# Attention scores from two-part float32r queries and keys, two heads per instruction pair, in a one-core attention and expert kernel

## The chip, the cores and the metric

The kernel runs on one core of one Trainium2 chip, in one launch. The metric is the device time of that core in microseconds (us), the median of a few runs. TensorE (PE) multiplies matrices, VectorE (DVE), ScalarE (ACT) and GpSimd (POOL) work on elements, SyncE (SP) issues most transfers. All data is float32 in DRAM unless said.

## The reference, cut to what matters

A token lookup, a layer norm, multi-head attention with a rotary part, a residual, and a layer with 32 experts of which each token takes one. The change is in how queries and keys are stored, and in the scores and their maxima:

```
query = heads(ct_q @ Wu_q_w + Wu_q_b) + heads(_rope(ct_q @ Wq_r_w + Wq_r_b, cos, sin))
key   = heads(ct_kv @ Wu_k_w + Wu_k_b) + heads(_rope(x @ Wk_r_w + Wk_r_b, cos, sin))
attn  = softmax(einsum('bhqd,bhkd->bhqk', query, key) / scale)
out   = einsum('bhqk,bhkd->bhqd', attn, value)
```

There are 4 sequences of 2048 tokens, 256 channels, and 16 heads of 16 channels each. The scores of one head are a 2048 by 2048 matrix whose inner dimension is only 16.

## The kernel before

Four phases follow each other. Phase A (lookup, norm, queries, keys, values) works in 16 chunks of 512 tokens. Phase B is the attention. Phase C is the output product, the second norm and the router; phase D the experts. The order of instructions on each engine is written out by hand, and semaphores join the engines. The change touches A and B.

**Phase A.** For each chunk PE makes the rotary part (`rotary`, L290 and L293), the latents of the next chunk (`latent`, L276) and the content part (`content`, L302). DVE adds them into `full` (L412), once for queries and once for keys. `full` is then split into three bf16 numbers whose sum is the float32 number: ACT rounds it to bf16 (L358), POOL subtracts that from `full` to give `rest` (L250), ACT rounds the rest (L360), and DVE subtracts again (`third`, L417). SP stores the three parts to DRAM (L192), six transfers for queries and six for keys per chunk.

**Phase B.** The unit of work is 4 heads (a quad) with 512 queries. For each unit the product runs over 16 blocks of 128 keys. One block for the 4 heads is called a group here: there are 8 units in a step and 8 steps, so 1024 groups, each with 4 tiles of 128 keys by 512 queries. Per group:

- `scores` (L718), 4 matmuls, one per head, bf16: the keys of a block are the stationary operand, the queries stream through. The exact float32 product is had from six products of bf16 parts (`PAIRS`), which stand one above another in the contraction: 6 times 16 rows, and 3 more rows that carry the negative maximum of each query, so 99 rows in all. The result goes to one of three PSUM banks `ps_s`.
- ACT takes the exponential of each tile (L791) out of `ps_s` into `probs`.
- `weigh` (L733), 4 float32 matmuls, one per head, each in its own 32 columns of the array: values by `probs`, added up in the bank `ps_o`. PE carries out a float32 matmul as two instructions, so the trace shows 8.
- `maximum` (L698), 4 matmuls, bf16, 96 rows: the same scores turned round, queries stationary, for the maxima of a unit further on; DVE takes the maximum over the 512 keys (L813) out of one of three banks `ps_m`. The maxima run `LEAD` = 80 tiles ahead of the scores.

Once per unit DVE joins the maxima (L821), POOL splits them in three bf16 parts (L647 to L653), PE transposes them (`turn`, L708) into a bank of its own, `ps_n`, ACT copies them out (L774), and SP writes them into three rows of the queries. Once per unit ACT also copies `ps_o` out (L780).

PE goes through its program in order, and a matmul waits until the bank that it writes is free. The order within a group is: score, maximum, score, maximum, and so on four times, then the `weigh` of the group before.

Of the kernel before, what the change touches and what calls it, by code (L numbers as in the profile page):

```python
# [7 lines left out]
F32 = mybir.dt.float32  # L21
BF16 = mybir.dt.bfloat16
# [5 lines left out]
P = 128  # L28
# [17 lines left out]
PAIRS = [(0, 0), (0, 1), (0, 2), (1, 0), (1, 1), (2, 0)]  # L46
SROWS = len(PAIRS) * HD
MROWS = SROWS + PARTS
QUAD = 4
# [22 lines left out]
def phase_a(nc, dram, out):  # L72

    with ExitStack() as ctx:
# [30 lines left out]
        rest = sb("rest", [P, 2, 2, CH])  # L105
        parts = sb("parts", [P, 2, 2, PARTS, 2, CH], BF16)
# [28 lines left out]
        part1_ok = [sem("part1_ok_q"), sem("part1_ok_k")]  # L135
        rest_ok = [sem("rest_ok_q"), sem("rest_ok_k")]
        part2_ok = [sem("part2_ok_q"), sem("part2_ok_k")]
        part3_ok = [sem("part3_ok_q"), sem("part3_ok_k")]
# [5 lines left out]
        STORES = 2 * 2 * PARTS  # L144
# [9 lines left out]
        with nc.Block() as block:  # L154
            @block.sync
            def _(sp):
# [14 lines left out]
                def chunk(b, k, last):  # L171
# [15 lines left out]
                    for x in range(2):  # L187
                        sp.wait_ge(part3_ok[x], after(b, k))
                        for g in range(PARTS):
                            for eo in range(2):  # L190
                                dst = dram["qk"][x][bass.ds(b * HEADS, HEADS), g, eo, :, k * CH:(k + 1) * CH]
                                sp.dma_start(dst, parts[:, par, x, g, eo, :]).then_inc(parts_out[par], 16)  # L192
# [13 lines left out]
            def _(pool):  # L206
# [25 lines left out]
                def chunk(b, k, last):  # L232
# [13 lines left out]
                    for x in range(2):  # L246

                        pool.wait_ge(part1_ok[x], after(b, k))
                        pool.wait_ge(part3_ok[x], b * CPB + k)
                        pool.tensor_tensor(rest[:, x], full[:, x], parts[:, k % 2, x, 0], ALU.subtract).then_inc(rest_ok[x], 1)  # L250
# [87 lines left out]
            def _(act):  # L338
# [15 lines left out]
                def split(b, k, x):  # L354
# [24 lines left out]
            def _(dve):  # L379
# [26 lines left out]
                def add_content(b, k, x):  # L406
# [3 lines left out]
                    dve.wait_ge(rest_ok[x], b * CPB + k)  # L410
# [20 lines left out]
                def chunk(b, k, first, last):  # L431
# [3 lines left out]
                    if not (first and k == 0):  # L435

                        third(*((b, k - 1) if k else (b - 1, CPB - 1)), 1)
# [18 lines left out]
                    third(b, k, 0)  # L456
                    add_content(b, k, 1)

                bv_twice = b_v[:].rearrange("p (a h d) -> p a h d", a=1, d=HD).to_broadcast([P, 2, HEADS, HD])
                for k in range(CPB):  # L460
                    chunk(0, k, True, False)
                with dve.Fori(1, BATCH - 1) as b:
                    for k in range(CPB):
                        chunk(b, k, False, False)
                for k in range(CPB):
                    chunk(BATCH - 1, k, False, True)
                third(BATCH - 1, CPB - 1, 1)


def phase_b(nc, dram, out):  # L470
# [3 lines left out]
    TILES = UNITS * KT * QUAD  # L474
    PER_UNIT = KT * QUAD
    STEPS = QUADS // 2
    LEAD = PER_UNIT + 16
# [3 lines left out]
    QT = CH // P  # L481
    KC = SEQ // 512

    with ExitStack() as ctx:
# [5 lines left out]
        keys = sb("keys", [P, 2, QUAD, SEQ], BF16)  # L490
# [52 lines left out]
        def total(ring):  # L543

            return [len(range(i, TILES, ring)) for i in range(ring)]

# [1054 lines left out]
```

## Time and profile before

| | |
|---|---|
| time, median of 3 runs | 3951.06 us (3947.47 to 3952.72) |
| profiled execution, its own time is its span | 4004.2 us |
| PE busy | 3682.7 us, 92% |
| DVE busy | 3108.8 us, 78% |
| ACT busy | 2340.3 us, 58% |
| phase A | from 0 to about 380 us |
| phase B | from about 380 to about 3400 us |
| phases C and D | the rest, about 600 us |

The profile is of one execution, which took 53 us longer than the median of the runs without a profile. "Busy" for PE takes in the model of how a matmul drains; two matmuls overlap in the trace, so the time from the start of one to the start of the next is the better measure of pace.

### The profile page before, as it was taken

The numbers are of one execution on the slowest core, as the hardware profiler recorded it, in microseconds if no ns is written. First come the engines' busy times: TensorE is split into PE (matmuls) and PEld (weight loads), VectorE is DVE, ScalarE is ACT, GpSimd is POOL, SyncE is SP. The second block draws the span as 40 slices with busy tenths as digits, with TensorE's granted clock in tenths as the row PEclk, the third lists the DMA queues.
The fourth block names the chain that finished last, engine by engine and source line by source line (L and its number), as shares of the span: only waits on it lengthen the run. The fifth ranks groups of instructions, "written<-read, shape, count | busy, mean of one in ns | idle before, by whom it ended". The sixth has DMA issues, their size and how long they took to land. (4 is left out here: it accounts for less than half of the span.)

```text
span 4004.2 us, 70540 instructions
## 1 busy us (share of the span) xinstructions
PE 3682.7 (92%) x19328; PEld 1342.4 (34%) x19328; DVE 3108.8 (78%) x5336; ACT 2340.3 (58%) x4484; POOL 646.8 (16%) x838
## 2 busy tenths in 40 slices
PE   6775999999999999999999999999999999575888
PEld 3432233323323322333233323322332332464555
DVE  6887988888888888888888888888888885575222
ACT  2322477777767776777677767767777777100111
POOL 5554000000000000000000000000000000355554
PEclk9887799999999999999999999999999999776999
DMA  5556202020202111120202020202112000466442
GB/s 152 171 161 170 42 22 50 21 54 13 55 13 57 26 44 38 30 44 24 45 27 54 12 55 12 54 13 59 29 38 44 23 15 15 137 198 190 146 141 85
DMA packets 268209, 258.28 MB, mean 65 GB/s; under 512 B 59140, under 2 KB 225581, under 8 KB 267601
## 3 DMA queue, kind: packets, MB, share of 16 engines
q1 hardware_dynamic: 252496, 224.42, 22.0%
q0 software_dynamic: 15360, 29.50, 2.6%
q8 instruction: 180, 2.95, 0.3%
q14 instruction: 173, 1.41, 0.1%
HBM read 159.56 MB, written 103.49 MB: 66 GB/s over the span
## 5 line engine op out<-in xcount | busy, mean ns | idle before, releaser
L813 DVE TENSOR_REDUCE max_parts<-ps_m 128x1 f32<-128x512 f32 x4096 | 2546.0, 683 | 394.2 <-PE ps_m L698 392.3
L791 ACT ACTIVATE probs<-ps_s 128x512 f32<-128x512 f32 x4096 | 2129.3, 603 | 811.9 <-PE ps_s L718 811.7
L698 PE MATMUL ps_m<-keys,queries 96*128 96x512 bf16 x4096 | 1580.7, 386 | 33.3 <-DMA queries<-split_q 32.9
L718 PE MATMUL ps_s<-queries,keys 99*128 99x512 bf16 x4096 | 1564.4, 383 | 31.5 <-issue 25.4
L733 PE MATMUL ps_o<-probs,vals 128*32 128x512 f32 x8192 | 1094.7, 606 | 0.3 <-ACT weighted L780 0.2
L718 PEld LDWEIGHTS ps_s<-queries,keys 99*128 99x128 bf16 x4096 | 397.1, 97 | 1301.8 <-issue 819.7
L698 PEld LDWEIGHTS ps_m<-keys,queries 96*128 96x128 bf16 x4096 | 400.0, 98 | 474.2 <-DVE max_parts L813 92.5
L659 POOL TENSOR_TENSOR heads_out<-weighted,recip_rows 128x512 f32<-128x512 f32 x64 | 81.3, 1270 | 2103.1 <-DMA recip_rows<-recip_rows_dram 2103.1
L733 PEld LDWEIGHTS ps_o<-probs,vals 128*32 128x32 f32 x8192 | 161.4, 108 | 371.3 <-issue 356.5
L1509 DVE TENSOR_TENSOR hidden<-ps_u,silu 128x320 f32<-128x320 f32 x64 | 30.9, 491 | 178.3 <-PE ps_u L1445 131.3
L647 POOL TENSOR_TENSOR neg_split<-neg_max,zeros_b 128x16 bf16<-128x16 f32 x64 | 14.1, 220 | 771.3 <-DVE neg_max L821 771.3
L1103 PE MATMUL ps_p<-w_o,att_t 128*128 128x256 f32 x256 | 88.8, 522 | 34.4 <-DMA att_t<-att 30.4
L1488 ACT ACTIVATE silu<-ps_g 128x320 f32<-128x320 f32 x64 | 27.2, 436 | 146.1 <-PE ps_g L1445 110.9
L268 PE MATMUL ps_t<-ident_a,normed 128*128 128x128 f32 x128 | 28.7, 398 | 84.5 <-DVE normed L394 84.5
L1156 ACT ACTIVATE rows_t<-ps_tc 128x1024 f32<-128x1024 f32 x16 | 16.4, 1023 | 144.9 <-PE ps_tc L1113 106.6
L1455 PE MATMUL ps_y<-w_down,hidden 128*64 128x256 f32 x640 | 92.1, 386 | 8.8 <-DVE hidden L1509 8.8
L250 POOL TENSOR_TENSOR rest<-full,parts 128x1024 f32<-128x1024 f32 x32 | 68.2, 2130 | 140.5 <-ACT parts L358 140.2
L1404 POOL DMA_INDIRECT out<-result,tokens_d x80 | 80.1, 1001 | 46.1 <-DVE result L1516 34.1
L1388 POOL DMA_INDIRECT rows_d<-rows,tokens_d x80 | 80.9, 1012 | 35.9 <-issue 22.3
L1482 ACT ACTIVATE rows_td<-ps_td 128x512 f32<-128x512 f32 (+1 forms) x48 | 24.7, 525 | 106.0 <-PE ps_td L1434 64.0
L1103 PEld LDWEIGHTS ps_p<-w_o,att_t 128*128 128x128 f32 x256 | 68.8, 276 | 50.3 <-issue 36.1
L1445 PE MATMUL ps_g<-rows_td,w_gate 128*128 128x320 f32 x256 | 84.6, 478 | 0.6 <-issue 0.6
(103 smaller groups left out, 1931.7 us busy)
## 6 DMA issues: line engine op xcount, KB each, us to landing
queries<-split_q SPq DMA_DIRECT2D x384, 64.0 KB
rows<-rows_c SPq DMA_DIRECT2D x16, 1032.0 KB, 6.4
vext<-val SPq DMA_DIRECT2D x64, 256.0 KB, 3.6
vals<-vext SPq DMA_DIRECT2D x32, 512.0 KB
recip_rows<-recip_rows_dram SPq DMA_DIRECT2D x64, 256.0 KB
att<-heads_out SPq DMA_DIRECT2D x64, 256.0 KB, 2.7
split_q<-parts SPq DMA_DIRECT2D x96, 128.0 KB
split_k<-parts SPq DMA_DIRECT2D x96, 128.0 KB
```

The costliest lines, as they stand in the source:

```text
L250: pool.tensor_tensor(rest[:, x], full[:, x], parts[:, k % 2, x, 0], ALU.subtract).then_inc(rest_ok[x], 1)
L659: pool.tensor_tensor(heads_out[:, lu % 2, :], weighted[:, lu % 2, :], recip_rows[:, lu % 2, :], ALU.mult).then_inc(heads_ok, 1)
L698: pe.matmul(ps_m[bank][:], queries[0:SROWS, par, qt, j, t * P:(t + 1) * P], keys[0:SROWS, par, j, c * 512:(c + 1) * 512], start=True, stop ...
L718: pe.matmul(ps_s[n % BANKS][:], keys[0:MROWS, par, j, k * P:(k + 1) * P], queries[0:MROWS, par, qt, j, :], start=True, stop=True).then_inc ...
L733: mm = pe.matmul(ps_o[32 * j:32 * j + 32, :], vals[:, par, k, VW * j:VW * (j + 1)], probs[:, (n + j) % RING, :], start=k == 0, stop=k == K ...
L791: act.activation(probs[:, n % RING, :], ps_s[n % BANKS][:], ACT.Exp, scale=SCALE).then_inc(probs_ok[n % BANKS], 1)
L813: dve.tensor_reduce(max_parts[:, lu % 2, g:g + 1], ps_m[bank][:], AX.X, ALU.max).then_inc(maxima_ok[bank], 1)
L1103: mm = pe.matmul(ps_p[:, t // 2, t % 2 * DM:(t % 2 + 1) * DM], att_t[:, k % 2, d, t * P:(t + 1) * P], w_o[:, d, :], start=d == 0, stop=d = ...
L1388: pool.indirect_dma_start(rows[:, k, i, :], None, dram["rows"], bass.IndirectOffsetOnAxis(ap=tokens[:, k, i:i + 1], axis=0), bounds_check= ...
L1404: pool.indirect_dma_start(out, bass.IndirectOffsetOnAxis(ap=tokens[:, k, i:i + 1], axis=0), result[:, k % 2, i, :], None, bounds_check=T - ...
L1445: mm = pe.matmul(bank[m][:, 0:CAP], w[:, k, KD * e + d, m * P:(m + 1) * P], by_half[:, :, e, :], start=d == 0, stop=d == KD - 1)
L1455: mm = pe.matmul(ps_y[n % 2][e * HALF:(e + 1) * HALF, 0:DM], hidden[:, k % 2, e, f, i * HALF:(i + 1) * HALF], w_down[:, k, (FF // P) * e + ...
```

## The change

In phase A `full` is split into two float32 numbers: ACT writes it rounded to the type float32r (a 32-bit word whose low mantissa bits are dropped), and POOL writes the exact rest. The second ACT pass, `rest` and `third` are gone; SP stores two parts of 4 bytes where it stored three of 2, four transfers for queries and four for keys per chunk.

In phase B the contraction is three products of parts (rest by high, high by high, high by rest), 48 rows, and 3 rows for the maximum, 51 in all, and matmuls read both operands as float32r. Head 0 of a pair lies at partitions 0 to 50, head 1 at 64 to 114, so the two matmuls of a pair use the upper and the lower 64 rows of the array and write different banks. Scores are issued in pairs (`score_pair`), which wait for both banks first. Maxima are issued in pairs too, into a double bank, and DVE takes the maximum of 2 times 512 in one instruction. `ps_m` is two double banks, so `ps_n` is gone, and `turn` takes its place in the ring of the three banks `ps_s` (`places`). The `weigh` of a group comes two groups later (`LAG` = 2), between the two score pairs. The maxima run 40 instruction pairs ahead. The rows of ones beside the keys are made by POOL in a small tensor and copied by 8 transfers, in place of a memset over 16384 columns.

```diff
 def phase_a
-                    act.activation(parts[:, k % 2, x, 0], full[:, x], ACT.Copy).then_inc(part1_ok[x], 1)
-                    act.wait_ge(rest_ok[x], after(b, k))
-                    act.activation(parts[:, k % 2, x, 1], rest[:, x], ACT.Copy).then_inc(part2_ok[x], 1)
+                    act.activation(parts[:, k % 2, x, 0].bitcast(F32R), full[:, x], ACT.Copy).then_inc(high_ok[x], 1)
...
-                        pool.wait_ge(part3_ok[x], b * CPB + k)
-                        pool.tensor_tensor(rest[:, x], full[:, x], parts[:, k % 2, x, 0], ALU.subtract).then_inc(rest_ok[x], 1)
+                        pool.tensor_tensor(parts[:, k % 2, x, 1].bitcast(F32R), full[:, x], parts[:, k % 2, x, 0], ALU.subtract).then_inc(low_ok[x], 1)
...
-                def third(b, k, x):
-                    dve.wait_ge(part2_ok[x], after(b, k))
-                    dve.tensor_tensor(parts[:, k % 2, x, 2], rest[:, x], parts[:, k % 2, x, 1],
-                                      ALU.subtract).then_inc(part3_ok[x], 1)
...
 def phase_b
-    LEAD = PER_UNIT + 16
+    LEAD = MAX_UNIT + 8
+    LAG = 2
     BANKS = 3
...
-                    pe.matmul(ps_m[bank][:], queries[0:SROWS, par, qt, j, t * P:(t + 1) * P],
-                              keys[0:SROWS, par, j, c * 512:(c + 1) * 512], start=True, stop=True).then_inc(maxima_ps, 1)
+                    for h in range(2):
+                        rows = slice(BASE * h, BASE * h + SROWS)
+                        mm = pe.matmul(ps_m[m % 2][:, h, :], queries_r[rows, par, qt, p, t * P:(t + 1) * P],
+                                       keys_r[rows, par, p, c * 512:(c + 1) * 512], start=True, stop=True)
+                    mm.then_inc(maxima_ps, 1)
...
-                    pe.wait_ge(probs_ok[n % BANKS], step * per_bank[n % BANKS] + n // BANKS)
+                    for i in (n, n + 1):
+                        pe.wait_ge(probs_ok[bank_of[i]], step * PER_BANK[bank_of[i]] + uses_before[i])
+                        if turn_before[i] is not None:
+                            pe.wait_ge(rows_ok, step * UNITS + turn_before[i] + 1)
...
+                    for h in range(2):
+                        rows = slice(BASE * h, BASE * h + MROWS)
+                        pe.matmul(ps_s[bank_of[n + h]][:], keys_r[rows, par, p, k * P:(k + 1) * P],
+                                  queries_r[rows, par, qt, p, :], start=True, stop=True).then_inc(scores_ok, 1)
...
-                        for i in range(QUAD):
-                            scores(step, n + i)
-                            if turns and i == 0:
-                                turn(step, lu + 1)
-                            if not (last and n + i + LEAD >= TILES):
-                                maximum(step, n + i)
-                        if n:
-                            weigh(step, n - QUAD)
+                        more = not (last and n // 2 + LEAD >= MAXIMA)
+                        if more:
+                            maximum(step, n // 2)
+                        if turns:
+                            turn(lu + 1, at[3][lu + 1][0])
+                        score_pair(step, n, at, first)
+                        if n >= LAG * QUAD:
+                            weigh(step, n - LAG * QUAD, at)
...
+                        if more:
+                            maximum(step, n // 2 + 1)
+                        score_pair(step, n + 2, at, first)
...
-                    dve.tensor_reduce(max_parts[:, lu % 2, g:g + 1], ps_m[bank][:], AX.X, ALU.max).then_inc(maxima_ok[bank], 1)
+                    dve.tensor_reduce(max_parts[:, lu % 2, :, p, t, c], ps_m[m % 2][:], AX.X, ALU.max).then_inc(maxima_ok[m % 2], 1)
```

On PE, in the middle of phase B, one group of before reads as follows, from one `weigh` (`ps_o`) to the next piece (bank numbers are those of `ps_s` and `ps_m`).

```order
L698 MATMUL ps_m1<-keys,queries 128x512
L718 MATMUL ps_s2<-queries,keys 128x512
L698 MATMUL ps_m2<-keys,queries 128x512
L733 MATMUL ps_o<-probs,vals 32x512 x4
L718 MATMUL ps_s0<-queries,keys 128x512
L698 MATMUL ps_m0<-keys,queries 128x512
L718 MATMUL ps_s1<-queries,keys 128x512
L698 MATMUL ps_m1<-keys,queries 128x512
```

In the changed kernel the same place reads so; `score_pair` is L738, `maximum` L706, `weigh` L753.

```order
L753 MATMUL ps_o<-probs,vals 32x512 x4
L706 MATMUL ps_m1<-keys,queries 128x512 x2
L738 MATMUL ps_s0<-queries,keys 128x512
L738 MATMUL ps_s1<-queries,keys 128x512
L706 MATMUL ps_m0<-keys,queries 128x512 x2
L738 MATMUL ps_s2<-queries,keys 128x512
L738 MATMUL ps_s0<-queries,keys 128x512
L753 MATMUL ps_o<-probs,vals 32x512 x4
```

What moved: `weigh` now stands between the first and the second score pair of a group, and the first pair after the second one needs two of only three banks, so a bank that the pair just before it has filled: in these rows the pair into banks 2 and 0 follows the pair into 0 and 1.

On DVE in phase A, the end of a chunk of before, where the key part of `full` is made:

```order
L387 BN_AGGR mv<-stats 128x2 x4
L454 TENSOR_TENSOR sums<-terms 128x512
L455 TENSOR_TENSOR sums<-terms 128x512
L417 TENSOR_TENSOR parts<-rest,parts 128x1024
L412 SCALAR_TENSOR_TENSOR full<-ps_r,b_cols,sums 128x512 x2
```

And in the changed kernel, where rows with ISA are waits:

```order
L370 BN_AGGR mv<-stats 128x2 x4
L428 ISA
L429 TENSOR_TENSOR sums<-terms 128x512
L430 TENSOR_TENSOR sums<-terms 128x512
L390 ISA
L391 ISA
L393 REGISTER_ALU
L395 SCALAR_TENSOR_TENSOR full<-ps_r,b_cols,sums 128x512 x2
```

The subtraction between `sums` and `full` is gone; nothing takes its place.

## Rows read from the trace of the kernel before

**Rows 1.** The page: span, busy time by engine, granted clock in 40 slices.

```profile
span 4004.2 us, 70540 instructions
PE 3682.7 (92%) x19328; PEld 1342.4 (34%) x19328; DVE 3108.8 (78%) x5336; ACT 2340.3 (58%) x4484; POOL 646.8 (16%) x838
...
PEclk9887799999999999999999999999999999776999
```

**Rows 2.** Windows: stretch, its length, busy time (instructions) by engine, PEclk, DMA share, GB/s.

```profile
100.00:200.00 100.00, 78.90 (x204) 40.18 (x205) 83.03 (x144) 30.45 (x33) 57.33 (x47) 0.90 0.59 171
420.00:440.00 20.00, 19.76 (x36) 3.55 (x35) 19.97 (x35) 0.27 (x1) 0.88 (x4) 0.50 0.00 0
...
600.00:700.00 100.00, 100.00 (x563) 30.09 (x562) 87.44 (x145) 73.51 (x145) 5.56 (x11) 1.00 0.24 49
3375.00:3398.00 23.00, 20.43 (x119) 4.45 (x118) 0.25 (x1) 20.02 (x40) 1.27 (x1) 1.00 0.07 25
```

**Rows 3.** Timeline of PE, mid phase B: start, duration, instruction, count.

```profile
700.64 0.38 PE L718 MATMUL ps_s<-queries,keys 99*128 99x512 bf16 x1
700.86 0.38 PE L698 MATMUL ps_m<-keys,queries 96*128 96x512 bf16 x1
701.17 1.06 PE L733 MATMUL ps_o<-probs,vals 128*32 128x512 f32 x8
702.17 0.39 PE L718 MATMUL ps_s<-queries,keys 99*128 99x512 bf16 x1
```

**Rows 4.** Timeline of ACT and DVE, the same stretch.

```profile
702.59 2.06 ACT L791 ACTIVATE probs<-ps_s 128x512 f32<-128x512 f32 x4 [0.78 <-PE ps_s L718]
...
702.81 2.48 DVE L813 TENSOR_REDUCE max_parts<-ps_m 128x1 f32<-128x512 f32 x4 [0.36 <-PE ps_m L698]
```

**Rows 5.** Groups by line and form: count, busy us, mean ns, idle before.

```profile
L813 DVE TENSOR_REDUCE max_parts<-ps_m 128x1 f32<-128x512 f32 x4096 | 2546.0, 683 | 394.2 <-PE ps_m L698 392.3
L791 ACT ACTIVATE probs<-ps_s 128x512 f32<-128x512 f32 x4096 | 2129.3, 603 | 811.9 <-PE ps_s L718 811.7
...
L698 PEld LDWEIGHTS ps_m<-keys,queries 96*128 96x128 bf16 x4096 | 400.0, 98 | 474.2 <-DVE max_parts L813 92.5 <-DVE ident_b L831 33.7 <-issue 5.3
...
L417 DVE TENSOR_TENSOR parts<-rest,parts 128x1024 bf16<-128x1024 f32 x32 | 39.0, 1218 | 5.8 <-ACT parts L360 5.8
...
L774 ACT ACTIVATE neg_rows<-ps_n 48x128 bf16<-48x128 bf16 x64 | 16.5, 257 | 66.7 <-PE ps_n L708 66.7
...
L1434 PEld LDWEIGHTS ps_td<-ident_d,rows_d 128*128 128x128 f32 x160 | 19.2, 148 | 64.0 <-issue 59.1 <-ACT rows_td L1482 1.8
```

**Rows 6.** Timeline of PE and ACT at the end of phase B, where no maxima are left.

```profile
3388.92 0.82 PE L718 MATMUL ps_s<-queries,keys 99*128 99x512 bf16 x3
...
3389.34 2.06 ACT L791 ACTIVATE probs<-ps_s 128x512 f32<-128x512 f32 x4 [0.33 <-PE ps_s L718]
...
3390.00 0.39 PE L718 MATMUL ps_s<-queries,keys 99*128 99x512 bf16 x1 [0.26 <-ACT probs L791]
3390.32 1.07 PE L733 MATMUL ps_o<-probs,vals 128*32 128x512 f32 x8
```

**Rows 7.** Timeline of DVE and PE in one chunk of phase A.

```profile
157.11 1.22 DVE L417 TENSOR_TENSOR parts<-rest,parts 128x1024 bf16<-128x1024 f32 x1
158.35 1.41 DVE L412 SCALAR_TENSOR_TENSOR full<-ps_r,b_cols,sums 128x512 f32<-128x512 f32 x2
...
152.81 3.60 PE L276 MATMUL ps_l<-normed_t,w_down_qkv 128*128 128x512 f32 x8
156.24 1.88 PE L302 MATMUL ps_r<-lat,w_uk 128*128 128x512 f32 x4
```

**Rows 8.** Timeline of DVE and PE at the start of phase B.

```profile
382.50 12.03 DVE L831 CAST ident_b<-ident_bf 128x128 bf16<-128x128 f32 x1 [8.88 <-DMA ident_bf<-in_ident]
...
395.32 1.01 PE L698 MATMUL ps_m<-keys,queries 96*128 96x512 bf16 x2 [32.90 <-DMA queries<-split_q]
```

More of the change, by code:

```diff
@@ L21 @@
 F32 = mybir.dt.float32
+F32R = mybir.dt.float32r
 BF16 = mybir.dt.bfloat16
@@ L429, in _, with chunk @@
                 dve.wait_ge(ones_set, 1)
-                def chunk(b, k, first, last):
+                def chunk(b, k, last):
                     rope_terms(b, k, 0)
@@ L455, in chunk @@
                     dve.tensor_tensor(sums[:, 1, 1, :], terms[:, 1, 2, :], terms[:, 1, 3, :], ALU.add).then_inc(sums_ok[1], 1)
-                    third(b, k, 0)
                     add_content(b, k, 1)
                 bv_twice = b_v[:].rearrange("p (a h d) -> p a h d", a=1, d=HD).to_broadcast([P, 2, HEADS, HD])
+                with dve.Fori(0, BATCH - 1) as b:
+                    for k in range(CPB):
+                        chunk(b, k, False)
                 for k in range(CPB):
[L461 to L467, printed above, removed]
+                    chunk(BATCH - 1, k, True)
 def phase_b(nc, dram, out):
@@ L480, in phase_b, with places @@
     SLOTS_PV = RING // QUAD
-    QT = CH // P
-    KC = SEQ // 512
+    TURN = 14
+    def places(last):
+        order = []
+        for n in range(TILES):
+            lu, k, j = n // PER_UNIT, n // QUAD % KT, n % QUAD
+            if k == TURN and j == 0 and not (last and lu == UNITS - 1):
+                order.append(("turn", lu + 1))
+            order.append(("tile", n))
+        bank_of, uses_before, turn_before, turn_bank = {}, {}, {}, {}
+        used, latest = [0] * BANKS, [None] * BANKS
+        for place, (kind, i) in enumerate(order):
+            bank = place % BANKS
+            if kind == "turn":
+                turn_bank[i] = bank, used[bank]
+                latest[bank] = i
+            else:
+                bank_of[i], uses_before[i], turn_before[i] = bank, used[bank], latest[bank]
+                used[bank] += 1
+                latest[bank] = None
+        return bank_of, uses_before, turn_before, turn_bank, used
+    PLACES = [places(False), places(True)]
+    PER_BANK = PLACES[0][4]
     with ExitStack() as ctx:
@@ L520, in phase_b @@
         maxima_ps = sem("maxima_ps")
-        maxima_ok = [sem(f"maxima_ok{i}") for i in range(BANKS)]
+        maxima_ok = [sem(f"maxima_ok{i}") for i in range(2)]
         neg_ok = sem("neg_ok")
@@ L609, in _ @@
                 load_vals(0, 0)
+                sp.wait_ge(ones_ok, 2)
+                for h in range(2):
+                    row = BASE * h + SROWS
+                    for par in range(2):
+                        for p in range(HP):
+                            sp.dma_start(keys[row:row + PARTS, par, p], ones[:]).then_inc(ones_in, 16)
                 max_rows(0, 0)
@@ L798, in step_of @@
                                 copy_weighted(step - 1, UNITS - 1)
+                        act.wait_ge(scores_ok, step * TILES + n + 1)
+                        if j == 0:
+                            act.wait_ge(pv_ok[n // QUAD % SLOTS_PV], step * (TILES // RING) + n // RING)
+                        act.activation(probs[:, n % RING, :], ps_s[bank][:], ACT.Exp, scale=SCALE).then_inc(probs_ok[bank], 1)
                 step_of(0, True, False)
@@ L1528, in build @@
 def build(nc, dram, out, phases="ABCD"):
+    dram["halves"] = [nc.dram_tensor(f"halves_{x}", (BATCH * HEADS, HALVES, 2, HD // 2, SEQ), F32, kind="Internal").ap() for x in "qk"]
     if "A" in phases:
```

210 lines of the change are left out of this document (107 added, 103 removed).

## The prediction, written before the changed kernel was run

> **What bounds the kernel now.** I read the page first. PE is busy for 92% of the span, DVE for 78%, ACT for 58%, and the granted clock is near full in all slices of the middle [rows 1]. The windows then split the span: between 600 and 700 us, inside phase B, PE is busy all the time at the full clock of 2.4 GHz, DVE for 87% and ACT for 74% [rows 2]. So there PE sets the pace. Each group has 16 PE instructions (4 scores, 4 maxima, 8 for `weigh`), and each 16 groups have one `turn`: 16.06 per group, and 563 in 100 us [rows 2] give 35.05 groups, so **2.853 us per group**.
>
> The timeline shows what the 2.85 us are made of. From one bf16 matmul to the next it is 0.22 us, from the last matmul to `weigh` 0.31 us (700.86 to 701.17), and from `weigh` to the next matmul 1.00 us (701.17 to 702.17) [rows 3]. Seven steps of 0.22 and these two make 2.85. The other two engines have room: 4 exponentials end to end take 2.06 us, and 4 maxima 2.48 us [rows 4]. With the single durations of 603 and 683 ns [rows 5], the step from one to the next is (2.06 - 0.60) / 3 = 0.487 us on ACT and (2.48 - 0.68) / 3 = 0.600 us on DVE.
>
> Phase A has another bound, a ring through all engines (its PE is busy for 79%, DVE for 83% [rows 2]).
>
> **The change in phase B, per group.** *DVE.* Two reductions of 1024 elements replace four of 512. No reduction of this shape stands in the trace. L417 handles 1024 elements on DVE in 1.218 us, against 0.683 us for the 512 of L813 [rows 5]: 0.535 us for the second half. So I take a step of 0.600 + 0.535 = 1.135 us, two per group, 2.27 us, and 2.30 us with the small work of each unit. Below this the group can't go: **the floor is 2.30 us**.
>
> *ACT.* Four exponentials as before, 4 times 0.487 = 1.95 us. Not the bound.
>
> *PE.* `weigh` is untouched, 0.31 and 1.00 us. The trace has no float32r matmul and no row tile. If the two matmuls of a pair run beside each other, and each streams 512 columns at the pace of the bf16 rows, a pair takes 0.22 us, and PE needs 0.22 x 2 + 0.31 + 1.00 + 0.22 = 1.97 us.
>
> That neither 1.97 nor 2.30 is the answer comes from the order and the three banks. The group is now: maxima, pair A, `weigh`, maxima, pair B. Three banks can't hold two pairs. The next pair A needs the two banks after those of B, and one of these holds the first tile of B. So it waits until ACT has read that tile, and everything on PE behind A, the `weigh` too, waits with it. The end of phase B, where the maxima are gone and PE waits for ACT in each group, gives the prices: from a score matmul to its exponential 3388.92 to 3389.34 = 0.42 us; from the start of the exponential to the matmul that wanted its bank, 3389.34 to 3390.00 = 0.66 us; to `weigh` 0.32 us [rows 6]. The ring of a group is then
>
> - B's first matmul to its exponential: 0.42
> - exponential to the first matmul of A: 0.66
> - first to second matmul of A: d
> - to `weigh` and out of it: 0.31 + 1.00
> - maxima pair, before B may start: 0.22
>
> which is 2.61 us + d. Is ACT free when B arrives? B's result comes 1.53 + 0.42 = 1.95 us after A's start, and A's two tiles have left ACT at 0.42 + 0.97 = 1.39 us: yes. Are the maxima ready? DVE needs 2.27 of 2.6 us, so they are; a delay there is no part of the ring.
>
> The term d is the time by which the second half of a pair trails the first when PE starts from a standstill, its weights being loaded after those of the first. Below, it is nothing, if the two loads overlap. Above, it is the load of 128 float32 columns, 148 ns at its shortest in the trace; the bf16 load takes 98 ns [rows 5]. I take the latter, nearer to a single pass over the weights: d = 0.10, and the range is 2.61 to 2.76 us.
>
> Where d is 0.15, the maxima pair behind `weigh` is also longer, two loads of 0.15 in place of 0.22, so the upper end is 2.84 us. I take 2.71 us, and for `turn`, which now takes a bank from the ring: before its pair can start, the second tile of B must have left ACT too, 0.487 us later than the first. That is 0.49 / 16 = 0.03 us per group. The copy of the turned rows, 0.257 us [rows 5], lies on ACT in that gap. **Together 2.74 us per group, 0.113 us less than 2.853.** Over the 1004 groups that have maxima beside them this is 113 us. The last 20 lose a little, the ring without maxima being 0.42 + 0.66 + 0.10 + 1.31 = 2.49 against 0.42 + 0.66 + 0.32 + 1.00 = 2.40 us before [rows 6]: 2 us back.
>
> Nearest to a row-tiled pair in the trace are the four column tiles of `weigh`, run beside each other, 8 instructions in 1.00 us [rows 3]. By the Trainium skill, TensorE: Matmul & The Clock Gate, Part 3 (packing small matmuls), the second matmul of a row-tiled pair starts about 4 ns after the first. With that d in place of my 0.10 the group would be 2.64 us and the time about 3727 us, my lower end; no run here shows it yet.
>
> *Lead-in.* The maxima before the first score are bound by DVE at 0.60 us each, 80 of them, 48 us. Now 40 at 1.135, 45 us: 3 us less. The cast of L831 took 12.03 us beside the memset on POOL, but PE's first matmul at 395.32 is put down to the queries' transfer [rows 8], which carries the same bytes; with half the descriptors of the queries I allow 3 us less.
>
> **The change in phase A.** `third` of the queries, 1.22 us on DVE, lies just ahead of `full` of the keys (157.11 to 158.33, `full` at 158.35). But `full` also needs the content matmuls, which start at 156.24 and end at 158.12 on PE [rows 7], whose place in the order does not change. So the subtraction hides beside PE, and its removal is worth some 0.2 us in each of 16 chunks: 3 us. Behind the last chunk an ACT pass and a `third` fall away before the stores end: 3 us. If PE were not late behind it, all 16 would give 1.2 us, 20 us in all. The stores grow from 6 to 8 bytes per number while 59% of the DMA time is taken [rows 2]; in fewer and larger pieces I cost them at nothing, and 5 us if that cover fails.
>
> **Sum.** -113 + 2 - 3 - 3 - 3 - 3 = -123 us. Against the profiled execution's 4004.2 us that is 3881 us. It ran 53 us over the median, and the terms are counts times paces, so I take them off the median: 3951 - 123 = **3828 us**, I say 3830.
>
> **The rivals.**
> - *The ring does not bind* (chance 0.04). ACT's release comes earlier than in the rows at the end, and DVE's floor rules: (2.853 - 2.30) x 1024 = 566 us less, 3370 us. Against it: the 1.08 us from matmul over ACT to matmul stands in the rows at the end [rows 6]. The Trainium skill speaks for it, page TensorEngine Tiling, section PSUM Bottleneck: tiling speeds up TensorE but not the reading of PSUM, which may become the bound; read as DVE's pace, that is this rival.
> - *The pair doesn't overlap* (chance 0.14): float32r at the bf16 pace, but one half after the other. Then d = 0.22 and the maxima pair takes 0.43: 0.42 + 0.66 + 0.22 + 1.31 + 0.43 + 0.03 = 3.07 us, 0.217 more over 1004 groups, 218 us, less 12 for the small terms: 4157 us, **slower**. It decides from d + the maxima pair over 0.43 us, since then 2.853 is reached. For it: 64-row halves occur nowhere in the trace. Against it: the four column tiles of `weigh` do overlap, 8 instructions in 1.00 us where one bf16 matmul takes 0.22.
> - *float32r costs more than one pass* (chance 0.09). In float32 each half of a matmul streams 0.43 us (L276, 8 in 3.60 us [rows 7]). If a pair takes 0.43 us in each place, three steps grow by 0.21 and the mean delay to ACT too: some 3.3 us per group, 4400 us. A page of the Trainium skill, FP8 and Floating Point Precision, section TensorE Precision Notes, calls true float32 four passes and names a mode that reads 4 bytes and truncates them; it gives no time for it, and no row here does.
> - *The clock* (chance 0.05). In the lead-in PE has one matmul for each 0.60 us of DVE, 0.43 us at half clock (twice the 0.22), and is held at half clock (0.50), while the end of phase B, with a pause of 0.26 us in each group, is at 1.00 [rows 2, 6]. After the change PE pauses for some 0.7 us per group. If phase B stayed at half clock, `weigh` alone would take 1.8 us, and the group about 4.2 us: over 5000 us.
>
> **How the numbers follow.** The ring with the pair side by side has 0.68; its own range is from d = 0 (2.64 us with `turn`: 3951 - 214 - 10 = 3727) to d = 0.15 with the longer loads (2.87 us: 3951 + 17 - 10, about 3960). To leave out no more than 2 in 10, the range must take in the serial pair at 4157 as well: 3725 to 4170 leaves out the floor of DVE, the slow passes and the clock, 0.18. A difference under 0.2%, 8 us, can't be told from none. Of the 0.68, 0.04 falls within 8 us of before and 0.01 above; the rest, and the 0.04 of the floor, are faster: 0.67. Same 0.04, slower 0.29.
>
> **What would show it.** L738 in pairs with starts about 0.1 us apart or less; on the waits, PE's L738 behind ACT for some 0.6 us once in each group, as the largest wait of PE; the reduction of 2 x 512 near 1.2 us with DVE busy for about 84% of phase B; `full` in phase A hardly earlier. Wrong would be: pairs 0.2 us apart or matmuls of over 0.4 us; DVE without gaps; PE without gaps; PEclk under 1.00 in the middle.

## The result, and the profile after

The changed kernel takes 4105.2 us (median of 4 runs, 4097.51 to 4122.64), against 3951.89 us before: a ratio of **1.039 (95% interval 1.0365 to 1.0418), slower**. The time lies inside the range of 3725 to 4170, but on the other side of no change than forecast.

The page of the changed kernel, answering to [rows 1] and [rows 5]:

```profile
span 4120.9 us, 65441 instructions
...
PE 3299.3 (80%) x19328; PEld 1348.8 (33%) x19328; DVE 2933.1 (71%) x3256; ACT 2415.2 (59%) x4452; POOL 638.4 (15%) x838
...
PEclk9897899999998999999999979898999999577799
...
L840 DVE TENSOR_REDUCE max_parts<-ps_m 128x2 f32<-128x1024 f32 x2048 | 2418.1, 1221 | 673.5 <-PE ps_m L706 667.4
...
L738 PE MATMUL ps_s<-queries,keys 51*128 51x512 f32 x4096 | 958.5, 463 | 540.0 <-ACT probs L825 487.0
```

No engine is full any more: PE fell from 92% to 80%, and its own largest wait in the table is for ACT to free a score bank, 487 us. The reduction of 2 x 512 takes 1221 ns (1.218 us was taken for it).

The timeline of PE in the middle of phase B, answering to [rows 3]:

```profile
1000.05 0.49 PE L738 MATMUL ps_s<-queries,keys 51*128 51x512 f32 x2 [0.45 <-ACT probs L825]
1000.48 1.06 PE L753 MATMUL ps_o<-probs,vals 128*32 128x512 f32 x8
1001.47 0.50 PE L706 MATMUL ps_m<-keys,queries 48*128 48x512 f32 x2
1001.81 0.40 PE L738 MATMUL ps_s<-queries,keys 51*128 51x512 f32 x2
1002.05 0.40 PE L706 MATMUL ps_m<-keys,queries 48*128 48x512 f32 x2
1002.89 0.49 PE L738 MATMUL ps_s<-queries,keys 51*128 51x512 f32 x2 [0.45 <-ACT probs L825]
```

And of ACT: the two tiles of pair A (which started at 1000.05), and the two of pair B (1001.81):

```profile
1000.66 1.08 ACT L825 ACTIVATE probs<-ps_s 128x512 f32<-128x512 f32 x2 [0.17 <-PE ps_s L738]
1002.24 1.09 ACT L825 ACTIVATE probs<-ps_s 128x512 f32<-128x512 f32 x2 [0.49 <-PE ps_s L738]
```

The two matmuls of a pair are one row, since they lie on each other (3 ns between their starts in the trace), and one pair follows another after 0.24 us (1001.81 to 1002.05). So in the middle of a run of pairs, one costs the array about what a single bf16 matmul did (0.22). The ring reads off as forecast: pair B at 1001.81, its exponential at 1002.24 (0.43), the next pair A at 1002.89 (0.65), `weigh` 0.43 behind it, the next maxima 0.99 behind that, pair B 0.34 on: **2.84 us**, where before had 2.85.

So the steady pace gained nothing, and something else cost time. The next rows are the timeline of PE at the start of a unit.

```profile
1059.93 0.40 PE L706 MATMUL ps_m<-keys,queries 48*128 48x512 f32 x2
1063.71 0.50 PE L738 MATMUL ps_s<-queries,keys 51*128 51x512 f32 x2 [3.38 <-DMA queries<-neg_rows]
...
1067.66 1.93 PE L753 MATMUL ps_o<-probs,vals 128*32 128x512 f32 x8
...
1072.16 1.93 PE L753 MATMUL ps_o<-probs,vals 128*32 128x512 f32 x8
```

PE stands for 3.4 us, until the rows with the maxima have landed in the queries. Then `weigh` takes 1.93 us in place of 1.06 and a group 4.50 us (1067.66 to 1072.16). The windows tell why, and that the end of phase B looks the same:

```profile
1055.00:1060.00 5.00, 4.46 (x32) 1.66 (x32) 3.53 (x4) 3.43 (x8) 0.00 (x0) 1.00 1.08 177
1060.00:1065.00 5.00, 1.62 (x14) 0.34 (x10) 2.25 (x2) 1.76 (x4) 0.00 (x0) 1.00 0.42 73
1065.00:1070.00 5.00, 4.75 (x22) 1.70 (x20) 2.36 (x2) 2.83 (x6) 0.00 (x0) 0.53 0.00 0
1070.00:1075.00 5.00, 4.74 (x20) 1.67 (x20) 2.50 (x3) 2.51 (x5) 0.00 (x0) 0.50 0.02 2
1075.00:1080.00 5.00, 4.27 (x30) 1.18 (x26) 4.32 (x4) 3.88 (x8) 0.00 (x0) 0.95 0.00 0
...
3510.00:3570.00 60.00, 48.38 (x176) 11.73 (x178) 0.25 (x1) 32.28 (x60) 1.27 (x1) 0.50 0.03 9
```

PEclk, the first number behind POOL's count, goes from 1.00 to 0.50, that is from 2.4 to 1.2 GHz, behind the pause, and comes back after some 10 us. In the last 60 us of phase B, where no maxima are left, it stays at 0.50; before had 1.00 there [rows 2].

SP's queue shows why the rows came late. It issued them as soon as ACT had copied them (1055.17); what is late are the loads ahead of them:

```profile
1033.54 0.33 SPq L599 DMA_DIRECT2D recip_rows_dram<-recip  x1
...
1042.18 0.34 SPq L560 DMA_DIRECT2D keys<-halves_k  x1
...
1052.79 0.32 SPq L568 DMA_DIRECT2D queries<-halves_q  x1
1055.20 1.61 SPq L588 DMA_DIRECT2D queries<-neg_rows  x2
```

The loads of the next quad's keys and queries are issued from 1042.18 to 1052.79 and keep the DMA engines full up to about 1062 (DMA share 1.08, then 0.42 in the windows above). The rows, issued at 1055.20, share the engines with them. In the kernel before the loads take the DMA engines as long, some 20 us, but they start 21.3 us before the first score of the next unit (1020.12 to 1041.45), and in the changed kernel 18.6 us before that score was due (1042.18 to about 1060.8). So there they are just done when the rows are needed, and its waits for these rows were short (1.2 us on the matmuls of L718 and 9.0 us on their loads over the whole run; 46.5 and 48.8 us on those of L738 after). The same view of before:

```profile
1011.40 0.33 SPq L594 DMA_DIRECT2D recip_rows_dram<-recip  x1
...
1020.12 2.58 SPq L557 DMA_DIRECT2D keys<-split_k  x3
1022.92 14.81 SPq L563 DMA_DIRECT2D queries<-split_q  x24
1037.87 1.82 SPq L583 DMA_DIRECT2D queries<-neg_rows  x3
```

From the denominators (1000.11 before, 1019.94 after) to the start of the key load it is 20.0 us before and 22.2 after, and the denominators themselves come a group later, because of `LAG` = 2. The reciprocals moved from group 5 to group 6 of the unit.

I took the start of the first `weigh` matmul of each group, from the first to the last but one: 2957.8 us before, 3128.4 after, 171 us more. Sorted by the distance between neighbours:

| part of phase B | before | after | difference |
|---|---|---|---|
| usual group | 2.847 | 2.841 | -6 |
| groups of 2.94 us, in the first and last step | none | 248 | +23 |
| groups with a `turn`, over the usual | 63 x 0.27 | 63 x 0.50 | +15 |
| pauses and half clock (groups over 3.46 us ahead of the last 19), over the usual | 39 | 147 | +107 |
| last 19 groups | 45.8 | 76.7 | +31 |

That is 170 of 171. Of the 147 us, 35 lie at the five ends of the loop over steps, where before has nearly all of its 39, and some 110 at the 12 places with late rows: pauses of 2.2 to 5.8 us, and behind them 69 us of half clock. Before phase B the change gained 2.7 us (it starts at 377.8, before at 380.5), and at the first score 1.6 us are left of it (441.2, before 442.8). Phases C and D, not changed, took 597 us in the profiled execution of before and 544 in that of after. I take these 53 us to lie in the executions and not in the kernels, since before's profile stood 53 us over its median; no second profile of before was taken to show it. The account agrees: phase B's 171 us less 1 us ahead of it, less the 16 us by which after's profile stood over its own median, is 154, and the medians differ by 153.

### The profile page after: what moved, and what is told of

It reads as the page before. It is cut to its first block and busy times, and to the rows that moved or that the text cites. A ratio compares the mean times of both kernels' runs of the same rounds, so it can differ in the third digit from the quotient of the medians.

```text
span 4120.9 us, 65441 instructions
## 1 busy us (share of the span) xinstructions
PE 3299.3 (80%) x19328; PEld 1348.8 (33%) x19328; DVE 2933.1 (71%) x3256; ACT 2415.2 (59%) x4452; POOL 638.4 (15%) x838
## 5 line engine op out<-in xcount | busy, mean ns | idle before, releaser
L840 DVE TENSOR_REDUCE max_parts<-ps_m 128x2 f32<-128x1024 f32 x2048 | 2418.1, 1221 | 673.5 <-PE ps_m L706 667.4
L825 ACT ACTIVATE probs<-ps_s 128x512 f32<-128x512 f32 x4096 | 2223.2, 595 | 861.2 <-PE ps_s L738 859.3
L738 PE MATMUL ps_s<-queries,keys 51*128 51x512 f32 x4096 | 958.5, 463 | 540.0 <-ACT probs L825 487.0
L753 PE MATMUL ps_o<-probs,vals 128*32 128x512 f32 x8192 | 1160.0, 636 | 2.1 <-issue 2.1
L706 PE MATMUL ps_m<-keys,queries 48*128 48x512 f32 x4096 | 957.0, 464 | 58.2 <-DMA queries<-halves_q 29.5
L738 PEld LDWEIGHTS ps_s<-queries,keys 51*128 51x128 f32 x4096 | 408.8, 193 | 1004.9 <-ACT probs L825 656.4
L706 PEld LDWEIGHTS ps_m<-keys,queries 48*128 48x128 f32 x4096 | 402.7, 193 | 1018.7 <-issue 931.2
L753 PEld LDWEIGHTS ps_o<-probs,vals 128*32 128x32 f32 x8192 | 165.1, 110 | 270.2 <-issue 267.3
L327 ACT ACTIVATE normed_t<-ps_t 128x1024 f32<-128x1024 f32 x16 | 16.4, 1023 | 155.9 <-PE ps_t L253 155.9
L235 POOL TENSOR_TENSOR parts<-full,parts 128x1024 fp32r<-128x1024 f32 x32 | 75.3, 2353 | 138.8 <-ACT parts L343 138.3
L386 DVE SCALAR_TENSOR_TENSOR terms<-ps_r,b_cols,cos_sb 128x512 f32<-128x512 f32 x64 | 47.7, 746 | 58.1 <-PE ps_r L278 44.5
```

Of the source, the lines that this page charges most:

```text
L235: pool.tensor_tensor(parts[:, k % 2, x, 1].bitcast(F32R), full[:, x], parts[:, k % 2, x, 0], ALU.subtract).then_inc(low_ok[x], 1)
L706: mm = pe.matmul(ps_m[m % 2][:, h, :], queries_r[rows, par, qt, p, t * P:(t + 1) * P], keys_r[rows, par, p, c * 512:(c + 1) * 512], start= ...
L738: pe.matmul(ps_s[bank_of[n + h]][:], keys_r[rows, par, p, k * P:(k + 1) * P], queries_r[rows, par, qt, p, :], start=True, stop=True).then_ ...
L753: mm = pe.matmul(ps_o[32 * j:32 * j + 32, :], vals[:, par, k, VW * j:VW * (j + 1)], probs[:, (n + j) % RING, :], start=k == 0, stop=k == K ...
L825: act.activation(probs[:, n % RING, :], ps_s[bank][:], ACT.Exp, scale=SCALE).then_inc(probs_ok[bank], 1)
L840: dve.tensor_reduce(max_parts[:, lu % 2, :, p, t, c], ps_m[m % 2][:], AX.X, ALU.max).then_inc(maxima_ok[m % 2], 1)
```

## The experiments

Theory R: the ring through the three score banks sets the pace. Theory S: the pauses and the half clock behind them come from the late rows. Theory C: the clock falls because PE has too little to do per group, by itself. Rivals: PE or the pairs are the bound (P), DVE is part of it (D). These runs were on three chips: before took 4042 us on chip 6 (e1 to e4), 4045 on chip 9 (e5 to e8), where the changed kernel took 4215, and 3950 on chip 1 (e9, e10), as in the first measurement. So ratios to before on the same chip are compared, and the parts of phase B.

**e1_order**

```diff
-                        if more:
-                            maximum(step, n // 2 + 1)
                         score_pair(step, n + 2, at, first)
+                        if more:
+                            maximum(step, n // 2 + 1)
```

> The changed kernel with one edit: the second score pair of a group comes before the second maxima pair, right behind `weigh`. Theory R (the ring of the three banks sets the pace: score matmul, exponential, score matmul, weigh, score matmul; 2.84 us in the changed kernel's trace): the 0.34 us of the maxima pair leave the ring, but the score pair now starts from the weights load behind `weigh`, from which a first exponential came 0.61 us later instead of 0.43, so 2.84 - 0.34 + 0.18 = 2.69 us per group in the middle, some 150 us less over 1004 groups, of which the late rows of the maxima take back up to 35 since the units are shorter: 3970 to 4000 us. Rival P (PE or the pairs themselves are the bound, the order is of no matter): 2.84 us per group, 4105 us as it was. Rival D (DVE is delayed by the maxima coming in a bunch): over 2.84 us, slower than 4105.

Measured: ratio 0.9875 (0.9854 to 0.9896), 3984.47 against 4042.04 us. The usual group took 2.61 us, in the first and the last step 2.70. Two lines swapped, with the same instructions, gain 5% of the changed kernel and make it 1.2% faster than before. P and D are out: work that no engine lost can't have been the bound. The groups over 3.46 us still cost 148 us over the usual, against 147 in the changed kernel: the shorter units leave the late rows later still, and single groups with a pause now take up to 10 us.

**e2_recip**

```diff
-                        if prev and g == 12:
+                        if prev and g == 8:
```

> The changed kernel with one number changed: DVE makes the reciprocals 4 reductions (2 groups) earlier in a unit, so that SP goes on 5.7 us earlier to the loads of the next keys and queries. Theory S (at two units of each step the rows of the maxima land behind 3 MB of those loads, PE stands for 3 to 5 us, the clock then falls to half and stays there for 3 to 8 groups of 4.49 us; 138 us over 2.84 in all, loop ends among them): the pauses at units 1 and 5 go, and the half clock behind them with it, 80 to 100 us less, 4005 to 4025 us. Rival C (the clock falls because PE has too little to do per group, with or without a pause): the pause alone goes, 3 us at 14 places, about 4065 us, and groups at 4.49 us stay. Rival N: the reciprocals do not hold SP, 4105 us.

Measured: ratio 1.0145 (1.0123 to 1.0166), 2.5% less than the changed kernel. The usual group stayed at 2.85 us. Phase B from first to last `weigh` fell from 3128 to 3024 us, and the groups over 3.46 us now cost 37 us over the usual instead of 147, of which 35 at the ends of the loop. SP's queue at the same place in the unit:

```profile
1019.39 0.33 SPq L599 DMA_DIRECT2D recip_rows_dram<-recip  x1
...
1028.01 0.34 SPq L560 DMA_DIRECT2D keys<-halves_k  x1
...
1040.22 0.32 SPq L568 DMA_DIRECT2D queries<-halves_q  x1
1046.77 1.61 SPq L588 DMA_DIRECT2D queries<-neg_rows  x2
```

The rows now go out 6.5 us behind the issue of the last load, and the window of 20 us around the next unit's start is undisturbed:

```profile
1045.00:1065.00 20.00, 16.46 (x113) 5.67 (x111) 16.21 (x14) 15.37 (x31) 0.00 (x0) 1.00 0.13 23
```

This shows S: with the pauses gone the half clock at those places is gone too, at the same PE work per group. C is out for the middle of phase B. What is left are the ends of the loop over steps, which before had too.

**e3_tail**

```diff
                         if more:
                             maximum(step, n // 2)
+                        else:
+                            filler(n, 0, True)
```

(and the same for the second place; `filler` waits for the last maxima to be read, then makes a pair of matmuls into `ps_m` that nobody reads)

> The changed kernel with PE doing a matmul pair into the idle maxima banks wherever the last step has no maxima left (extra work whose result nobody reads; the output is unchanged). Theory C2 (the last 20 groups ran at half clock, 4.16 us each, because PE had too little to do; before they took 2.40 at full clock): with the filler the clock stays full and a group takes 2.84 us, 20 x 1.3 = 26 us less, about 4078 us. Rival: the fall had another cause, the filler makes each of the 20 groups longer by 0.3 to 0.6 us, 4110 to 4117 us.

Measured: ratio 1.0364 (1.0317 to 1.0411), not to be told from the changed kernel's, and the interval is as wide as the effect that was forecast. In the trace the last 19 groups took 55 us in place of 77, with the clock at 1.00:

```profile
3490.00:3550.00 60.00, 48.99 (x331) 17.49 (x329) 9.84 (x10) 44.76 (x85) 3.43 (x6) 1.00 0.05 16
```

So more work on PE made those groups shorter, and C holds there in this: the extra work keeps the clock up. The gain of 22 us is that of one execution. How long the clock lasts without it is not set by the work in a group alone. At full clock such a group takes 2.70 us, at half clock 4.16, and of the last 19 none was at full clock in the changed kernel's trace, 3 in e4's, 5 in e5's and 9 in e1's.

**e4_combined** has the edits of e1 and e2 (not shown again), and the loads spread over three units, which was not run by itself:

```diff
-                            load_stacks(step * 2 + (q + 1), 1 - q)
-                        if lu % 4 == 1 and not (last and q == 1):
+                            load_keys(step * 2 + (q + 1), 1 - q, stacks_in[1 - q])
+                            load_queries(step * 2 + (q + 1), 1 - q, 0, stacks_in[1 - q])
+                        if lu % 4 == 1 and not (last and q == 1):
+                            for qt in range(1, SEQ // CH):
+                                load_queries(step * 2 + (q + 1), 1 - q, qt, stacks_in[1 - q])
+                        if lu % 4 == 2 and not (last and q == 1):
```

> The order of e1, the early reciprocals of e2, and the loads of the next keys and queries spread over three units instead of two. R and S together: 2.69 us per group and no pause at units 1 and 5: 4105 - 150 - 90 = 3865 us, faster than before by 2%. If S is wrong, no better than e1; if R is wrong, no better than e2; under C groups at 4.49 us stay and the time is over 3920 us.

Measured: ratio 0.960 (0.9576 to 0.9623), as R and S together give. Of the groups over 3.46 us only those at the ends of the loop are left, 31 us. The timeline of PE shows the ring without the maxima:

```profile
1000.49 0.50 PE L742 MATMUL ps_s<-queries,keys 51*128 51x512 f32 x2
1000.83 0.75 PE L710 MATMUL ps_m<-keys,queries 48*128 48x512 f32 x4
1001.75 0.50 PE L742 MATMUL ps_s<-queries,keys 51*128 51x512 f32 x2 [0.17 <-ACT probs L829]
1002.18 1.06 PE L757 MATMUL ps_o<-probs,vals 128*32 128x512 f32 x8
1003.18 0.49 PE L742 MATMUL ps_s<-queries,keys 51*128 51x512 f32 x2
```

Both maxima pairs lie between B and A, where PE waited before, and A still comes by the exponential of B's first tile. The group here is 2.69 us; the median over phase B is 2.61.

This trace also prices a pair that finds its weights loaded. Where DVE holds up the second maxima pair, the score pair behind it has no wait, and its weights are loaded while the maxima stream. Its rows, PE and then the load:

```profile
1861.02 0.40 PE L742 MATMUL ps_s<-queries,keys 51*128 51x512 f32 x2
1861.36 1.06 PE L757 MATMUL ps_o<-probs,vals 128*32 128x512 f32 x8
...
1860.93 0.19 PEld L742 LDWEIGHTS ps_s<-queries,keys 51*128 51x128 f32 x2
```

The load starts 0.09 us ahead of the matmul, and `weigh` follows 0.34 us behind it. Of the pairs ahead of a `weigh` in this trace, 42 had their load begin 84 to 105 ns ahead, and `weigh` came after some 0.33 us (under 0.345); in 957 load and matmul began together, and it came after 0.42 to 0.45 us.

**e5_split_max**

```diff
-                    dve.tensor_reduce(max_parts[:, lu % 2, :, p, t, c], ps_m[m % 2][:], AX.X, ALU.max).then_inc(maxima_ok[m % 2], 1)
+                    for h in range(2):
+                        red = dve.tensor_reduce(max_parts[:, lu % 2, h:h + 1, p, t, c], ps_m[m % 2][:, h], AX.X, ALU.max)
+                    red.then_inc(maxima_ok[m % 2], 1)
```

> The changed kernel with one part undone: DVE takes the maximum of 512 elements twice in place of 2 x 512 once, everything else as it is. Theory R (the ring through the three score banks sets the 2.84 us; DVE waits in each group): DVE's work rises from 2.27 to 4 x 0.60 = 2.40 us, still under 2.84, so nothing moves: the ratio to before within 0.3% of that of the changed kernel on the same chip. Rival D (DVE is part of the bound): 0.13 us x 1024 = 130 us, 3% more.

Measured: 1.0388 (1.0358 to 1.0419), against 1.0409 (1.0384 to 1.0434) of the unaltered kernel beside it: the same. The usual group is 2.848 us in both, though DVE again has 4096 reductions of 684 ns (2548.3 us busy in place of about 2418). The joined maxima, one of the change's parts, are worth nothing in this kernel.

**e8_changed_again** is the base for it.

> The changed kernel unaltered, on the chip of the other three, as the base for e5: a ratio to before of 1.036 to 1.042, 2.84 us per group, late rows at units 1 and 5.

Measured: 4215.13 against 4044.51 us, 1.0409: the slowdown repeats on another chip.

**e6_banks4**

```diff
-    BANKS = 3
+    BANKS = 4
+    MB = 3
...
-        ps_m = [ctx.enter_context(nc.psum_tensor(f"ps_m{i}", [P, 2, CH], F32)) for i in range(2)]
+        ps_m = [ctx.enter_context(nc.psum_tensor(f"ps_m{i}", [P, CH], F32)) for i in range(MB)]
...
                     for h in range(2):
+                        bank, used = max_place(step, n, h)
+                        if not (n < 0 and 2 * m + h < MB):
+                            pe.wait_ge(maxima_ok[bank], used)
```

(with the early reciprocals and the spread loads of e4, so that e2's 1.0145 is the nearest to compare)

> The changed kernel with a fourth score bank, paid for by the maxima: they go through three single banks with a reduction of 512 each. The order in a group is that of the changed kernel; early reciprocals and spread loads as in e4, so that the loads do not disturb. Theory R: with four banks a pair waits for the pair before the last one, 0.61 + 0.49 + 0.66 = 1.76 us after that one's start, so the ring is gone; DVE's 4 x 0.60 us are next, 2.40 to 2.60 us per group against 2.84: about 3.5% to 6% faster than before with the stalls gone. Rival P (PE or the pairs are the bound): 2.84 us per group as in e2, the ratio 1.01.

Measured: 1.030 (1.0259 to 1.0342), a miss. The usual group got longer, 2.94 us. The timeline of PE:

```profile
1002.97 0.50 PE L721 MATMUL ps_m<-keys,queries 48*128 48x512 f32 x2
1003.31 0.40 PE L753 MATMUL ps_s<-queries,keys 51*128 51x512 f32 x2
1003.54 0.40 PE L721 MATMUL ps_m<-keys,queries 48*128 48x512 f32 x1
1004.25 0.50 PE L721 MATMUL ps_m<-keys,queries 48*128 48x512 f32 x1 [0.31 <-DVE max_parts L857]
1004.43 0.55 PE L753 MATMUL ps_s<-queries,keys 51*128 51x512 f32 x2
1004.92 1.06 PE L768 MATMUL ps_o<-probs,vals 128*32 128x512 f32 x8
```

The wait for a score bank is gone, and the same kind of ring has formed on the maxima banks: with three single banks the second half of a pair needs the bank that the pair just before it filled, so it waits for DVE (1002.97 to 1004.25), and `weigh` waits behind it. I had moved the ring, not removed it. In the middle the run neither confirms nor refutes R as it was meant to; it shows that any wait ahead of `weigh` counts. It does confirm R at the end of phase B, where no maxima are left and only the score banks matter. There ACT works without a gap, and the last 19 groups took 40 us, 2.1 us each, where three banks gave 2.70 at full clock; the clock stayed up, with no filler:

```profile
3485.00:3530.00 45.00, 40.51 (x265) 11.87 (x261) 2.27 (x5) 42.61 (x85) 2.16 (x5) 1.00 0.04 14
...
3499.58 6.78 ACT L840 ACTIVATE probs<-ps_s 128x512 f32<-128x512 f32 x13
```

**e7_combined_tail** is e4 with the filler of e3.

> e4 with the filler matmuls of e3 in the last groups, which ran at half clock in e4's trace (3.9 us each over the last 19). If PE's load per group is what holds the clock, they take 2.7 to 3.0 us: some 20 us less than e4, 0.5%. If not, 5 us more than e4.

Measured: 0.9522 (0.9497 to 0.9548) against e4's 0.960. The last 19 groups took 51 us in place of 74, at a clock of 1.00.

**e9_tile_waits**

```diff
-                    for i in (n, n + 1):
-                        pe.wait_ge(probs_ok[bank_of[i]], step * PER_BANK[bank_of[i]] + uses_before[i])
...
                     for h in range(2):
+                        i = n + h
+                        pe.wait_ge(probs_ok[bank_of[i]], step * PER_BANK[bank_of[i]] + uses_before[i])
```

(with the early reciprocals of e2)

> e2 (the changed kernel with early reciprocals) with the wait of a score pair split: each half waits for its own bank only. The ring then goes through the second half alone (the first tile of pair B frees the bank of the second half of the next pair A), and the first half, its weights too, is in the array before. Theory R with the pair's load as the oversize (0.43 us from A to weigh where 0.31 stood behind single matmuls): 2.84 falls by 0.05 to 0.11 us per group, 1% to 2.5% under e2's ratio of 1.0145. Rival: the halves must start together to run beside each other and the second takes its own 0.22 us longer: 2.84 us or more, the ratio of e2 or above.

Measured: 1.0101 (1.0084 to 1.0118), 0.4% under e2 on another chip, not the 1% to 2.5% of the theory. The usual group stayed at 2.846 us; only the groups of 2.94 us went, to 2.85. The rows:

```profile
1001.51 0.40 PE L738 MATMUL ps_s<-queries,keys 51*128 51x512 f32 x1
1002.11 0.50 PE L738 MATMUL ps_s<-queries,keys 51*128 51x512 f32 x1 [0.21 <-ACT probs L825]
1002.54 1.06 PE L753 MATMUL ps_o<-probs,vals 128*32 128x512 f32 x8
```

One lone half, its partner started 0.6 us before, is still followed by `weigh` after 0.43 us. So the 0.11 us over the bf16 kernel's 0.32 [rows 6] do not belong to the second half of the pair; with the rows of e4 they belong to a float32r matmul that starts with its weights not yet loaded. The end of this run has no filler, and the first 13 of its last 19 groups still ran at full clock, at 2.61 us, with PE in small pauses all the time; then the clock fell:

```profile
3400.00:3416.00 16.00, 13.27 (x73) 3.83 (x73) 0.00 (x0) 12.74 (x26) 1.27 (x1) 0.99 0.09 33
3416.00:3432.00 16.00, 14.96 (x49) 3.94 (x48) 0.00 (x0) 8.16 (x17) 0.00 (x0) 0.50 0.00 1
```

**e10_best** is e7 with the same split wait.

> e7 with the same split wait. Theory R: 2.61 falls by 0.05 to 0.11 us, the ratio from 0.952 to 0.925 to 0.94. Rival as in e9: 0.95 or above.

Measured: **0.9465 (0.9449 to 0.9481)**, 3738.94 against 3949.80 us, the fastest version. The group stays at 2.61 us, now in all steps; the forecast of 0.925 to 0.94 is missed for the same reason as in e9.

## Why the prediction was wrong, step by step

- **The ring** was the right mechanism, and it binds: shown by e1, which shortens it without taking work from any engine, and by the end of e6, where a fourth bank undoes it. Its size was off. I had 2.71 us and it measures 2.84: the maxima pair ahead of B takes 0.34 instead of 0.22 us, and from A to `weigh` it is 0.43 instead of 0.41. The failed term is the price of a float32r matmul that meets an unloaded array: I took the load for 0.10 us and counted it once; it is about 0.11 and occurs twice, behind the wait and behind `weigh`. That it is the unloaded array, and neither the second half of the pair nor the `weigh` beside it, is shown by e9 and by the rows of e4: the 42 pairs with their load ahead go on to `weigh` after 0.33 us. The loads of L738 are 193 ns long on average, against 98 for bf16; that their length is the 0.11 us is argued, not shown. By my own condition, no gain from d and the maxima pair over 0.43 us together, the pace was lost: they measure 0.12 (the 0.43 from A to `weigh`, less 0.31) + 0.34 = 0.46. I had written the double case down as the upper end (2.84 us) and put the middle below it. In the sum, 0.13 us x 1004 = 130 us, more than the whole forecast gain.
- **`turn`**, 0.49 us: measured 0.50, so the term was right. Before has 0.27 of its own, which its 2.853 held already.
- **The step that I left out: SP's queue.** I followed the change on PE, ACT and DVE, and not the moved `weigh` and reciprocals on to SP. `LAG` = 2 and g = 12 delay the denominators and reciprocals, behind which SP issues 3 MB of loads, and these meet the rows of the maxima. Pauses and half clock cost 107 us more than before, and e2, which starts the loads earlier, takes 110 us of them away. The slack of this transfer was small before, and its row stood in the table of waits.
- **The clock** was a rival at 0.05 for all of phase B, over 5000 us. In the steady middle it stayed at 1.00, with PE idle for a fifth of the time. It fell behind each of the 12 pauses and, in the last 20 groups, by itself, 31 us. So the rival was wrong as put and right in two places; e3 and e7 show that more work on PE prevents the second, and e6 that a pace without the ring's waits does too.
- **DVE's floor**: the price of the reduction was right (1.221 for 1.218 us), and e5 shows that it doesn't bind in the changed kernel.
- **The pair side by side**: right. The row tiles overlap with 3 ns between starts, behind a wait too. The Trainium skill (TensorE: Matmul & The Clock Gate, Part 3) has about 4 ns, and the trace agrees. So d, the trailing of the second half, was next to nothing, and the cost that I had put there sits between the pair and what follows it.
- **Phase A**: right. `third` is gone and `full` of the keys starts at 158.33 in place of 158.35 [rows 7], now waiting 1.15 us for PE's L287. The start of phase B came 2.7 us earlier, for the forecast 6. The lead-in, from the first maximum to the first score, was to save 3 us and took 1.2 longer (392.5 to 441.2, before 395.3 to 442.8).
- **The chances**, 0.67 on faster, were wrong because the two effects that cost most, together 130 us of ring and 138 us of pauses and clock (107 and 31), were given little chance or none. The range held the time only through the serial pair, which did not happen; that it held it was luck.

What stays open: why the clock falls in the last groups of the changed kernel, sooner in some runs than in others, and not in those of before, which have the same `weigh` and as many score matmuls, one behind the other instead of in pairs; and the 0.09 us between ACT and PE that the first and last step have over the others, which e9 removed and only that.

## What to carry to other kernels

Cheaper matmuls gain nothing when the order and the buffers tie them into a ring: write down the ring from result to release to next use, with all that the in-order engine still does inside it, and move work from the ring into the wait. Here two swapped lines did that: with the order of the changed kernel the pairs gained 0.006 us per group, with the new order 0.24. No run has the new order with bf16 matmuls; in before PE had no idle time in mid phase B [rows 2], so I would expect little of it there. Follow every delayed step on to the queue that issues transfers behind it: 12 pauses of 2 to 6 us on TensorE cost another 3 to 11 us each through the clock, 69 us in all.

## What the runs showed of the hardware

- A float32r pair of 51 x 512 in two row tiles of 64 follows the next after 0.24 us at full clock, as a single bf16 matmul of 96 x 512 did after 0.22.
- Behind a wait or a `weigh` the same pair takes 0.34 us; the bf16 matmul took 0.22 or 0.23. From such a pair to the first matmul of `weigh` it is 0.43 us, and 0.33 where its weights were loaded beforehand (e4); the bf16 matmul took 0.32 and 0.31.
- POOL's subtraction into float32r took 2353 ns, 2130 ns into float32 before.
- After each of 12 pauses of 2.2 to 5.8 us the granted clock went from 2.4 to 1.2 GHz and slowed two to seven groups; behind the one of 3.4 us shown above PE was busy for 4.75 of 5 us meanwhile.
- The same kernel took 2.3 to 2.4% longer on two chips than on another (before, 4042 and 4045 against 3950 us). For the changed kernel the difference lies behind phase B: from its first to its last `weigh` it took 3128 us in the first measurement and 3123 on chip 9, and from there to the end 543 and 645 us. The ratio to before was nearly the same, 1.039 and 1.041.
